# Output projection of an attention kernel: from three split f16 products to one f32 product per block

## What is computed

```python
y = ln(x).reshape(b, t, 16, 8).transpose(0, 2, 1, 3)      # 16 heads of size 8
attn = softmax(einsum('bhtk,bhsk->bhts', y, y) / sqrt(8))
o = einsum('bhts,bsc->bhtc', attn, ln(x))                 # every head weighs all 128 channels
x = x + ln(o.transpose(0, 2, 1, 3).reshape(b, t, 16 * 128) @ weight)
x = x + ln(ffn(ln(x), W_r, W_k, W_v, mu_r, mu_k))         # token shift, sigmoid gate, squared relu
```

## Time and profile before

| | |
|---|---|
| median of 3 timed runs | 979.81 us |
| the profiled execution | 983.67 us |
| its span | 981.9 us |
| mean granted clock of TensorE | 0.985 of full |
| busy: TensorE, VectorE, ScalarE, GpSimd | 913.7, 858.7, 761.7, 311.3 us |
| instructions | 17700 |

### The profile page before, as it was taken

The page is one execution under the profiler, slowest core; times in us unless marked ns, Lnnn a source line. Parts: engine busy times, 40 slices in busy tenths (PEclk is TensorE's granted clock), DMA queues, the critical chain, the costliest instruction groups (busy, mean ns, idle before and its releaser), DMA issues.

```text
span 981.9 us, 17700 instructions
## 1 busy us (share of the span) xinstructions
PE 913.7 (93%) x5979; PEld 439.2 (45%) x5979; DVE 858.7 (87%) x1125; ACT 761.7 (78%) x1045; POOL 311.3 (32%) x490
## 2 busy tenths in 40 slices
PE   4799999999999899999998989999999999999982
PEld 2244444444444344444444444444444444444452
DVE  6789998799799898888898899979979898898976
ACT  5777878877887688878877679787787878788864
POOL 2113211441145421543126531265114451164210
PEclk9999999999999999999999999999999999999996
DMA  5899999989898779899897898889988997989830
GB/s 166 175 222 195 207 189 208 207 187 193 169 182 178 160 155 184 184 222 206 170 179 160 166 183 164 180 197 195 208 166 177 185 190 159 186 168 193 168 62 22
DMA packets 99465, 173.50 MB, mean 177 GB/s; under 512 B 21296, under 2 KB 62128, under 8 KB 99376
## 3 DMA queue, kind: packets, MB, share of 16 engines
q0 software_dynamic: 36720, 133.71, 70.9%
q1 hardware_dynamic: 62464, 38.54, 14.3%
q10 hardware_dynamic: 192, 0.13, 0.1%
HBM read 28.12 MB, written 10.49 MB: 39 GB/s over the span
## 4 chain that ended last, share of the span: by engine, by line
PE 65%; POOL 9%; ACT 8%; issue 7%; DVE 7%; DMA 3%; ACTq 0%; DVEq 0%; POOLq 0%
PE ps_o L587 18%; PE ps_o L588 16%; PE ps_o L589 16%; POOL fnw L387 6%; PE ps_s L568 6%; ACT e_f L747 5%; DVE e_lo L1083 2%; DMA e_hi<-e_f 2%; PE ps_r L604 2%; PE ps_r L603 2%; PE ps_r L602 2%; POOL e_hi L422 1%; POOL nw L387 1%; ACT L747 1%; ACT part L764 1%
## 5 line engine op out<-in xcount | busy, mean ns | idle before, releaser
L1083 DVE TENSOR_TENSOR e_lo<-e_f,e_hi 128x2048 f16<-128x2048 f32 x256 | 585.6, 2288 | 64.4 <-DMA e_hi<-e_f 62.8
L747 ACT ACTIVATE e_f<-ps_s 128x2048 f32<-128x2048 f32 x256 | 481.6, 1881 | 143.6 <-PE ps_s L568 135.9
L587 PE MATMUL ps_o<-e_hi,y_hi 128*128 128x512 f16 x1024 | 393.0, 384 | 9.3 <-DVE o_neg L1089 9.2
L588 PE MATMUL ps_o<-e_lo,y_hi 128*128 128x512 f16 x1024 | 390.5, 381 | 0.0
L589 PE MATMUL ps_o<-e_hi,y_lo 128*128 128x512 f16 x1024 | 390.1, 381 | 0.0
L422 POOL DMA_DIRECT2D e_hi<-e_f x255 | 139.1, 545 | 608.2 <-ACT e_f L747 551.3
L587 PEld LDWEIGHTS ps_o<-e_hi,y_hi 128*128 128x128 f16 x1024 | 100.0, 98 | 160.7 <-issue 60.5
L764 ACT ACTIVATE part<-ps_r,rden 128x128 f32<-128x128 f32 x508 | 144.3, 374 | 32.0 <-DVE rden L1095 32.0
L589 PEld LDWEIGHTS ps_o<-e_hi,y_lo 128*128 128x128 f16 x1024 | 100.7, 98 | 122.6 <-issue 2.8
L588 PEld LDWEIGHTS ps_o<-e_lo,y_hi 128*128 128x128 f16 x1024 | 100.7, 98 | 92.8 <-issue 2.9
L568 PE MATMUL ps_s<-op_t,op_s 32*128 32x512 f16 x1024 | 102.6, 388 | 25.4 <-ACT e_f L747 23.6
(11 more groups left out here) (216 smaller groups left out, 463.0 us busy)
## 6 DMA issues: line engine op xcount, KB each, us to landing
e_hi<-e_f POOLq DMA_DIRECT2D x255, 512.0 KB, 4.9
op_t<-scr_t SPq DMA_DIRECT2D x500, 32.0 KB, 3.6
op_s<-scr_s SPq DMA_DIRECT2D x504, 16.0 KB, 3.2
scr_s<-yT SPq DMA_DIRECT2D x12, 256.0 KB, 4.8
scr_t<-yT SPq DMA_DIRECT2D x12, 256.0 KB, 4.7
out_dram<-res SPq DMA_DIRECT2D x7, 256.0 KB, 4.8
xs<-in_L_attn_x_dram SPq DMA_DIRECT2D x3, 512.0 KB, 6.6
scr_s<-eighth SPq DMA_DIRECT2D x4, 256.0 KB, 4.0
```

The costliest lines, as they stand in the source:

```text
L587: nc.tensor.matmul(dst, y_hi[:, b % 2, s, :], e_hi[:, ring, g, :], start=(q == 0 and g == 0), stop=False)
L588: nc.tensor.matmul(dst, y_hi[:, b % 2, s, :], e_lo[:, ring, g, :], start=False, stop=False)
L747: nc.scalar.activation(e_f[:, k % EF_RING], ps_s[:], ACT.Exp, scale=1.0 / ROOT).then_inc(weighed, 1)
L1083: dve.tensor_tensor(flat(e_lo[:, ring]), flat(e_f[:, k % EF_RING]), flat(e_hi[:, ring]), ALU.subtract).then_inc(split, 1)
```

## The change

The projection multiplies f32 by f32. ScalarE copies the output out of PSUM into o_f in f32, without a factor. VectorE's second rounding is gone, in the loop and after it. TensorE makes one f32 matmul per block in place of three f16 ones. The weights are only centred, into a tile of their own, w_f; the sum of squares, the scale, the split into w_hi, w_lo and w_neg and all waits for them are gone, and the first layer norm's epsilon is the plain constant. TensorE's waits for o_split become waits for taken. The order of everything else is the same.

```diff
-        w_hi = sb("w_hi", [P, H, C], F16)
-        w_lo = sb("w_lo", [P, H, C], F16)
-        w_neg = sb("w_neg", [P, H, C], F16)
+        w_f = sb("w_f", [P, H, C], F32)
...
-        o_hi = sb("o_hi", [P, 2, BANK], F16)
-        o_neg = sb("o_neg", [P, 2, BANK], F16)
+        o_f = sb("o_f", [P, 2, BANK], F32)
...
             def products(k):
...
-                    ge(pe, o_split, j - 1)
+                    ge(pe, taken, j - 1)
...
             def project(j):
-                pe.wait_ge(o_split, j + 1)
+                pe.wait_ge(taken, j + 1)
...
-                    nc.tensor.matmul(dst, o_hi[:, j % 2, here], w_hi[:, j % H, :], start=True, stop=False)
-                    nc.tensor.matmul(dst, o_hi[:, j % 2, here], w_lo[:, j % H, :], start=False, stop=False)
-                    mm = nc.tensor.matmul(dst, o_neg[:, j % 2, here], w_neg[:, j % H, :], start=False, stop=True)
+                    mm = nc.tensor.matmul(dst, o_f[:, j % 2, here], w_f[:, j % H, :], start=True, stop=True)
...
-                nc.scalar.activation(o_hi[:, j % 2, :], ps_o[:, j % 2, :], ACT.Copy,
-                                     scale=2.0 ** -O_BITS).then_inc(taken, 1)
+                nc.scalar.activation(o_f[:, j % 2, :], ps_o[:, j % 2, :], ACT.Copy).then_inc(taken, 1)
...
             for k in range(LAST):
-                if k == 4:
-                    keep_weight_sum()
...
-                    square_weights()
-                if k == 5:
-                    weights_high()
-                if k == 7:
-                    weights_neg()
...
-                if (k - LAG - 3) % 2 == 0 and 0 <= j < LAST_STEP:
-                    split_o(j)
...
-                if k == 5:
-                    weight_scale()
-                if k == 6:
-                    weights_low()
...
-            for u in range(HALVES):
-                last_split(u)
```

More of the change, by code:

```diff
@@ L146, in sandwich @@
         x_half = sem("x_half")
[L147 removed]
+        w_based, w_marked = (sem(s) for s in ("w_based", "w_marked"))
         w_less, f_turned, f_ready = (sem(s) for s in ("w_less", "f_turned", "f_ready"))
@@ L163, in sandwich @@
         scored, weighed, split = (sem(s) for s in ("scored", "weighed", "split"))
-        product, taken, o_split, projected = (sem(s) for s in ("product", "taken", "o_split", "projected"))
+        product, taken, projected = (sem(s) for s in ("product", "taken", "projected"))
         den_ok, scaled, added = (sem(s) for s in ("den_ok", "scaled", "added"))
@@ L175, in sandwich @@
         f_gated, f_normed, y_out, stored = (sem(s) for s in ("f_gated", "f_normed", "y_out", "stored"))
-        w_sub = xs[:, 2 * NB:4 * NB, :]
-        l_taken, l_split, l_projected, l_inverted, l_scaled, l_added, l_full = (
-            sem(f"l_{s}") for s in ("taken", "split", "projected", "inverted", "scaled", "added", "full"))
+        l_taken, l_projected, l_inverted, l_scaled, l_added, l_full = (
+            sem(f"l_{s}") for s in ("taken", "projected", "inverted", "scaled", "added", "full"))
         l_sum = [sem(f"l_sum_{i}") for i in range(3)]
@@ L444, in mark_weights @@
             def mark_weights():
-                nc.gpsimd.memset(w_lo[:, :, C - 1:C], 0.0)
-                nc.gpsimd.tensor_scalar(w_hi[:, :, C - 1:C], ident[:, P - 1:P].unsqueeze(1).to_broadcast([P, H, 1]),
-                                        2.0 ** W_BITS, None, ALU.mult).then_inc(w_marked, 1)
+                nc.gpsimd.tensor_scalar(w_f[:, :, C - 1:C], ident[:, P - 1:P].unsqueeze(1).to_broadcast([P, H, 1]), 1.0, None,
+                                        ALU.mult).then_inc(w_marked, 1)
             pool.wait_ge(const_ok, 1)
@@ L681, in last_project @@
                     dst = half_ps("project", u)[:, i * P:(i + 1) * P]
-                    nc.tensor.matmul(dst, o_hi[:, LAST_STEP % 2, here], w_hi[:, H - 1, :], start=True, stop=False)
-                    nc.tensor.matmul(dst, o_hi[:, LAST_STEP % 2, here], w_lo[:, H - 1, :], start=False, stop=False)
-                    mm = nc.tensor.matmul(dst, o_neg[:, LAST_STEP % 2, here], w_neg[:, H - 1, :], start=False, stop=True)
+                    mm = nc.tensor.matmul(dst, o_f[:, LAST_STEP % 2, here], w_f[:, H - 1, :], start=True, stop=True)
                 mm.then_inc(l_projected, 1)
@@ L766, in scale @@
                 ins.then_inc(scaled, 1)
[L768 to L777, removed]
             def square_batch(b):
@@ L1055, in weight_base @@
                 step(dve.tensor_copy(col, raw[:, :, C - 1:C]))
-                dve.tensor_tensor(w_sub[:, 4 * i:4 * i + 4, 0:C - 1], raw[:, :, 0:C - 1],
+                dve.tensor_tensor(w_f[:, 4 * i:4 * i + 4, 0:C - 1], raw[:, :, 0:C - 1],
                                   col.to_broadcast([P, 4, C - 1]), ALU.subtract).then_inc(w_based, 1)
[L1059 to L1064, removed]
-                step(dve.tensor_scalar(ws[:, 2:3], ws[:, 1:2], ws[:, 1:2], EPS, ALU.mult, ALU.mult))
-                dve.tensor_scalar(ws[:, 2:3], ws[:, 2:3], 1e-30, None, ALU.max).then_inc(w_scale, 1)
-                dve.tensor_scalar(ws[:, 1:2], ws[:, 1:2], 2.0 ** W_BITS, None, ALU.mult).then_inc(w_scale, 1)
-                dve.wait_ge(w_scale, 2)
-            def weights_low():
-                dve.wait_ge(w_high, 1)
-                dve.wait_ge(w_scale, 2)
-                dve.scalar_tensor_tensor(out=w_lo[:, :, 0:C - 1], in0=w_sub[:, :, 0:C - 1], scalar=ws[:, 1:2],
-                                         in1=w_hi[:, :, 0:C - 1], op0=ALU.mult, op1=ALU.subtract).then_inc(w_split, 1)
             def split_quad(k):
@@ L1084, in split_quad @@
                                   ALU.subtract).then_inc(split, 1)
-            def split_o(j):
-                dve.wait_ge(taken, j + 1)
-                ge(dve, projected, j - 1)
-                dve.scalar_tensor_tensor(out=o_neg[:, j % 2, :], in0=o_hi[:, j % 2, :], scalar=2.0 ** O_BITS,
-                                         in1=ps_o[:, j % 2, :], op0=ALU.mult, op1=ALU.subtract).then_inc(o_split, 1)
             def invert(j):
@@ L1281, in last_root @@
                 dve.wait_ge(l_mean[i], count)
-                step(dve.tensor_scalar(v, l_mv[:, i, here, 1], ws[:, 2:3] if i == 0 else consts[:, 0:1], None, ALU.add))
+                step(dve.tensor_scalar(v, l_mv[:, i, here, 1], consts[:, 0:1], None, ALU.add))
                 dve.wait_ge(l_sqrt[i], 1 if here == ALL else count)
```

45 lines of the change are left out of this document (6 added, 39 removed).

## The result

| | before | after |
|---|---|---|
| median of 4 timed runs | 979.56 us | 992.45 us |
| the profiled execution | 983.67 us | 991.74 us |
| its span | 981.9 us | 989.9 us |
| start of the first projection | 49.73 | 48.49 |
| start of the 127th projection | 953.02 | 961.58 |

The ratio is 1.0143, 95% interval 1.0098 to 1.0188. With more runs of both on another chip it was 1.0148 (1.0122 to 1.0174). The changed kernel is slower by some 13 us; the two profiled executions alone differ by 8.1.

The account below looks back on a forecast made before the run. TensorE's own stream was taken as the bound. Matmuls +35.6, second rounding -5, waits for the exponential -9 and start -1.5 made +20.1 us on 979.8, so 999.9, predicted as 1000.0 us, range 991 to 1014.

Parts of the forecast that it names:

- the f32 group that costs less in its new place: Projection behind a 512-column product: first loads hidden longer, group 0.22 us over f16, 992.3 us in all; chance 0.05.
- the forecast proper: Whole kernel: slower by 20.1 us, with part of TensorE's waits returned; chance 0.73.
- the prediction's own sign: Interval between projections: 7.00 us in place of 6.72 if right; any other value means the matmul term is mis-sized.
- The bound: Loop: TensorE's own stream sets the ordinary 6.72 us step; 32.8 us of its waits are all that could come back.
- The projection's matmuls: Projection: 4 f32 matmuls in place of 12 f16 ones cost 0.28 us more in each of 127 steps, +35.6 us.
- The second rounding: VectorE in the loop: removing 127 operations returns 5 us of TensorE's 9.2 us of waits, between 0 and 9.2.
- The slack of the longer step: TensorE's 22 waits for the exponential: each shrinks by some 0.4 us, giving 9 us, between 0 and 23.6.
- a rival's price: In "VectorE's relief pays for all": some 3 us counted where TensorE ran slower behind two other long waits.
- The start: Before the loop: the weights' dropped preparation lets TensorE's products resume earlier, a gain of 1.5 us, between 0 and 3.
- nothing comes back: Loop waits: GpSimd and DMA landings set them, and o_neg waits become exponential waits; 1013.9 us with the start; chance 0.15.
- VectorE's relief pays for all: Loop and start: VectorE's lighter load returns all 32.8 us of waits and more, 38.8 against 35.6, 976.6 us; chance 0.05.
- The f32 weight loads that nothing hides: Projection: f32 weight loads aren't hidden, at least 0.8 us more in each of 127 steps, 1102 us; chance 0.02.

Follow-up runs that it names:

- 16 f32 parts: The changed kernel with each f32 projection matmul made twice: 1088.9 us, ratio 1.1123 to the kernel before.
- the second run: The changed kernel run once more, unaltered, on another chip: 992.54 us, ratio 1.0148 to the kernel before.
- the two half changes: Changed kernel with a VectorE operation of the old rounding's shape kept per step, 997.83 us; kernel before without the second rounding, still 12 f16 matmuls, 974.18 us.

## Why the prediction came out as it did

The forecast was 1000.0 us, slower, with 991 to 1014 as its range. 992.45 is inside, 1.5 us from the lower end, and the sign was right. It lies where one of the rivals, the f32 group that costs less in its new place, had put it (992.3, given a chance of 0.05); the forecast proper had 20.1 us more where 13 were measured. That rival came true, and by the prediction's own sign (an ordinary interval other than 7.00 us) its term of the matmuls was wrong. By its steps:

**The bound.** Right. The ordinary step was TensorE's stream, and it moved with the number and form of its matmuls: 6.27, 6.49, 6.72, 6.94, 7.83 us for 4, 8, 12 f16 matmuls, 8 and 16 f32 parts. But the 32.8 us of waits weren't "all that a lighter VectorE or ScalarE could give back inside the loop": 5.9 of them lie ahead of the first projection, and the waits for the layer norm (1.2 us) and the two stretches at a lower clock, which came with waits, aren't among the 32.8.

**The projection's matmuls, +35.6 us.** This term was mis-sized, and it is the whole miss as far as the medians can tell. The ordinary step grew by 0.22 us and not 0.28: 127 x 0.22 = 27.9 us, 7.7 less than forecast. The step that failed is the reading of the earlier trace rows as the price of the group. Both stand behind 128-column f16 matmuls, and the division of 1.11 - 0.28 by 7 spread one longer first gap (0.165 us, the other six 0.111 or 0.112) over all seven. The group's new neighbour, a 512-column product, was in the code; the prediction named this as a rival and gave it 0.05. The Trainium skill's rule of the half rate (Perfetto Trace Analysis, section Engine Utilization) gave an estimate of 0.111 us for a part, which is what the changed kernel measures. The prediction had put the rows over it, and the rows were of another neighbourhood.

**The second rounding, -5 us.** Right in size: 5.3 us at the f32 length and 4.4 at the f16 length, out of 9.2 of waits and 86.5 of VectorE's busy time. Right in the main in its reason: behind the same late queue a wait for o_neg turned in part into others. But in the longest case, 3.02 us, half of it moved to the layer norm (0.59 to 2.10 us) and only 0.85 to an exponential. VectorE's busy time fell by 72 us and not by the forecast 90: its records alone add up to 92.9 us less, but they overlap each other, and busy time counts an overlap once.

**The slack of the longer step, -9 us.** Right in size within the precision: four more f16 matmuls, the run that changes nothing else, stream 27.9 us more and cost 17.1, so 10.8 came back. The f32 group with the rounding kept cost 19.2, 8.7 less than its stream, but about 1 us of that is its earlier start, which leaves 7 to 8. The reason was right in part. The forecast let each of 22 waits for the exponential shrink by 0.4 us. They shrank to 19 waits and 17.7 us with four more matmuls, 5.9 us in all, and 5.5 more came from the waits for o_neg, which a longer step shortens too. The clock, which stood in the prediction only in a rival's price, had a share too: two stretches of 3.4 us at half the full clock in the profiled execution before, none in either run with the rounding kept. If TensorE loses half of such a stretch, that is 3.4 us (an estimate); over the timed runs, whose mean granted clock is 0.985 before and 0.987 there, it is nearer 2.

Part of the slack can be read interval by interval: the step of the feed-forward's key takes 8.51 us in the kernel before and in the changed one, and as much in the undisturbed cases with 4 and 8 f16 matmuls; only with 16 f32 parts does TensorE's stream pass it, at 8.69. There are six such steps, so this explains some 1.3 us of it. The timeline of the kernel before has this at one such step:

```profile
362.73 1.28 ACT L747 ACT_TABLE_LOAD   x1
364.02 1.88 ACT L747 ACTIVATE e_f<-ps_s 128x2048 f32<-128x2048 f32 x1
...
365.95 0.40 PE L568 MATMUL ps_s<-op_t,op_s 32*128 32x512 f16 x4 [0.81 <-ACT e_f L747]
```

and that of the changed kernel at the same step of the same row:

```profile
366.69 0.39 PE L546 MATMUL ps_s<-op_t,op_s 32*128 32x512 f16 x4 [0.64 <-ACT e_f L719]
```

ScalarE loads a table after the sigmoid, the exponential comes behind it, and TensorE waits 0.81 us before and 0.64 after: up to that wait, a longer projection costs such a step nothing.

**The start, -1.5 us.** Right: the first projection came 1.24 us earlier (1.27 in the second run). TensorE didn't stay fast with it, as the upper end of 3 us would have needed: the granted clock is 0.50 from 41.3 to 48.1. The end was 0.5 us closer behind the last projection in the first profiled execution and not in the second, so it gave nothing that can be told from scatter. ScalarE's copy cost nothing more, and nobody waited for it anew.

**The sum** 27.9 - 5.3 - 8.7 = +13.9 us equals the difference of the medians (992.54 - 978.6), but it proves nothing: 5.3 and 8.7 are differences along the way from one median to the other, so they have to add up. A sum from runs off that way does test the terms: 27.9 of stream, less 10.8 of slack (four more f16 matmuls), less 4.4 for the rounding (12 f16 matmuls without it), less 1.2 for the start is +11.5 us against 13.9. The differences are uncertain by some 3 us each, so the two agree. No large errors of opposite sign hid each other; one term was off and the rest held. The profiled executions differ by only 8.1 us. The one before was slow for its kernel (983.67 us; on the two other chips of the first eight runs it took 973.7 to 984.3, with medians of 978.6 and 979.4), and its two stretches at half the clock can account for some 3.4 of these 5 us. What else is in it stays open.

Of the other rivals, "nothing comes back" and "VectorE's relief pays for all" are both refuted by the two half changes: relief gives 5 of the 36 us that the latter would need. The f32 weight loads that nothing hides (1102 us) are refuted by the eight parts at 0.111 us.

## What to carry to other kernels

An f32 matmul that replaced three f16 ones of 128 columns was not cheaper on TensorE: it has two parts of twice the length each, four f16 matmuls' worth. Where TensorE isn't the bound the trade may pay, which no run here shows. In this kernel, where TensorE bounds nearly every step, its added or saved time passes into the total by a share that falls as the step shortens: 85% from 8 to 16 f32 parts, 66% from 12 f16 matmuls to the f32 group (both without the rounding, the earlier start within), 60% from 12 to 8 and 27 to 42% from 8 to 4. The rest goes into waits and into TensorE's lower granted clock. Read the price of an instruction from a row that has the same neighbours as its new place, and look at the minimum and maximum of the line besides the mean.

## What the runs showed of the hardware

- A 128x128 by 128-column f32 matmul is recorded as two parts, 0.111 us apart, against 0.0555 us for an f16 matmul of that shape. The first part behind a 128-column f16 matmul is 0.053 us longer (328 ns against 275); behind a 512-column f16 matmul or another f32 part it is not.
- A wait of 2.97 us on TensorE cost more than itself in the kernel with 4 f16 matmuls: the stretch behind it ran at a granted clock of 0.54, and the step took 5.6 us more with both. Not every such wait does it: behind the 3.02 us at 330.34 in the kernel before, the clock was 1.00 from 330.3 to 333.7. The longest intervals between projections are 11.94 us with 4 f16 matmuls, 11.82 and 13.39 with 8, 10.57 in the kernel before, 9.63 and 11.05 in the changed one, and 8.72 with 16 f32 parts.
- The mean granted clock of the timed runs fell with TensorE's stream, from 0.989 with 16 f32 parts to 0.974 with 4 f16 matmuls.
- VectorE's 72 us less of busy time were answered by more idle, among it the waits for the casts' transfers, 62.8 to 86.1 us.
